# Two attention layers and two routed expert layers on one core: statistics behind the first maximum, a query product by halves, the sums of batch 3 later, and the lane tiles of the second routing on VectorE

## The reference, cut to what matters

```python
x = x + L0_xattn(layernorm(x), ctx)   # one head; softmax over ctx, a second softmax over the row maxima
x = x + L0_ffn(layernorm(x))          # 12 gates, 8 experts of 256 -> 512 -> 256 (silu), top 2
x = x + L1_xattn(layernorm(x), ctx)   # 4 heads of 64, mask, softmax over 1024, Wo
x = x + L1_ffn(layernorm(x))          # 8 experts of 256 -> 1024 -> 256 (gelu), top 2

# L1_xattn
q = layernorm(x) @ Wq;  k, v = split(ctx @ Wkv)
a = softmax(where(mask, q @ k.T * 64 ** -0.5, -inf));  out = (a @ v) @ Wo

# both ffn blocks: route by the two largest of logits = layernorm(x) @ gate
out = sum over the 2 experts picked of gate_weight * expert(layernorm(x))
```

## Time and profile before

| | |
|---|---|
| median of 3 runs | 990.28 us (989.05 to 993.0) |
| the profiled execution, time / span | 988.45 us / 986.4 us |
| mean granted clock of TensorE in it | 0.965 |
| busy share of PE, DVE, ACT, POOL | 90%, 63%, 54%, 44% |

### The profile page before, as it was taken

The page is one execution under the profiler, slowest core; times in us unless marked ns, Lnnn a source line. Parts: engine busy times, 40 slices in busy tenths (PEclk is TensorE's granted clock), DMA queues, the critical chain, the costliest instruction groups (busy, mean ns, idle before and its releaser), DMA issues. The chain is left out here.

```text
span 986.4 us, 19692 instructions
## 1 busy us (share of the span) xinstructions
PE 891.9 (90%) x6194; PEld 788.2 (80%) x6195; DVE 624.0 (63%) x1390; ACT 527.9 (54%) x1131; POOL 431.4 (44%) x374
## 2 busy tenths in 40 slices
PE   5899999858999997689999998986799999999995
PEld 4798988737999986478787787875389999999995
DVE  6975452585666666778787787866565444544452
ACT  5644140453444443686686776656755554555452
POOL 1474341006566663664263462210145555555542
PEclk9999999979999999889999999997799999999998
DMA  9631000457676739410010100009946666666762
GB/s 302 229 96 43 1 1 1 135 202 256 222 230 237 255 112 238 86 44 23 22 44 22 44 1 2 27 1 285 324 157 198 184 211 207 199 189 203 210 187 35
DMA packets 70707, 134.74 MB, mean 137 GB/s; under 512 B 8144, under 2 KB 52816, under 8 KB 65520
## 3 DMA queue, kind: packets, MB, share of 16 engines
q1 hardware_dynamic: 57296, 110.27, 33.7%
q0 software_dynamic: 13344, 23.63, 10.2%
HBM read 109.08 MB, written 21.64 MB: 133 GB/s over the span
## 5 line engine op out<-in xcount | busy, mean ns | idle before, releaser
L1840 ACT ACTIVATE x<-d_hps,b 128x128 f32<-128x128 f32 x312 | 89.0, 367 | 114.3 <-PE d_hps L1942 114.1
L1942 PEld LDWEIGHTS d_hps<-d_xg_t,d_xw 128*128 128x128 f32 x1248 | 145.1, 192 | 2.4 <-issue 1.0
L1942 PE MATMUL d_hps<-d_xg_t,d_xw 128*128 128x128 f32 x1248 | 145.5, 275 | 0.8 <-issue 0.8
L887 POOL TENSOR_SCALAR c_prob<-c_prob,c_rinv 128x1024 f32<-128x1024 f32 x64 | 72.0, 1142 | 125.3 <-DVE c_rinv L1348 124.9
L1952 PE MATMUL d_yps<-d_w,d_hid_hi 128*128 x312 | 115.2, 402 | 0.8 <-DVE d_hid_lo L2135 0.8
L1748 POOL DMA_INDIRECT out_x<-d_y,d_take_slot x39 | 63.6, 1630 | 106.2 <-DMA out_x<-d_y,d_take_slot 82.9
L2126 DVE TENSOR_SCALAR d_xg_t<-d_take,ln_w,ln_b 128x128 f32<-128x128 f32 x78 | 28.4, 406 | 93.0 <-PE d_take L1931 92.8
L1355 DVE TENSOR_TENSOR c_pt_lo<-c_tp,c_pt_hi 128x512 fp32r<-128x512 f32 x128 | 82.1, 682 | 5.2 <-ACT c_pt_hi L1177 4.9
L1341 DVE CUSTOM_DVE_ANT_0 c_prob<-c_sc,c_minf 128x1024 f32<-128x1024 f32 x64 | 75.6, 1218 | 11.3 <-PE c_sc L974 11.2
L1177 ACT ACTIVATE c_pt_hi<-c_tp 128x512 fp32r<-128x512 f32 x128 | 69.8, 597 | 22.1 <-PE c_tp L987 21.7
L987 PE MATMUL c_tp<-const,c_prob 128*128 128x128 f32 x512 | 70.5, 281 | 12.0 <-DVE c_pt_lo L1355 11.9
(11 more groups left out here) (377 smaller groups left out, 2209.5 us busy)
## 6 DMA issues: line engine op xcount, KB each, us to landing
d_xw<-in_w SPq DMA_DIRECT2D x39, 1024.0 KB
b_w<-in_w SPq DMA_DIRECT2D x47, 512.0 KB, 7.7
d_w<-in_w SPq DMA_DIRECT2D x8, 1024.0 KB, 12.0
a_raw<-in_ctx_t SPq DMA_DIRECT2D x8, 512.0 KB, 7.2
a_raw<-in_ctx SPq DMA_DIRECT2D x8, 512.0 KB, 4.5
ybuf<-a_zero SPq DMA_DIRECT2D x2, 2048.0 KB, 12.5
k_stage<-in_ctx_t SPq DMA_DIRECT2D x12, 256.0 KB, 3.2
rows<-b_xn_all SPq DMA_DIRECT2D x1, 2048.0 KB, 12.8
```

The lines of the kernel that those rows point to most:

```text
L887: nc.gpsimd.tensor_scalar(prob[w][:], prob[w][:], rinv[:, w:w + 1], 1.0, ALU.mult, ALU.mult).then_inc(s["prob_ready"], 1)
L1840: op = nc.scalar.activation(hid[q][:, h * FH + c, :], src[:, c, :], ACT.Gelu_apprx_tanh, bias=b1[:, ds(e, 1), h * FH + c])
L1942: mm = nc.tensor.matmul(hps[j % 2][h][:, c * P:(c + 1) * P], w1[j % WL][:, k, at:at + P], xg_t[j % 2][:, k, :], start=(k == 0), stop=(k == ...
```

## The change

Five edits. In attention0, `maximum(0, 0)` moves ahead of the last four `bn_stats`, the variance behind `invert(0, 0)`, the inverse deviation behind `maximum(0, 2)`, and ACT's root behind `exponential(0, 1)`. In attention1, SP waits for the second half of batch 0's rows before it loads batch 1's; 17 unread matmuls stand in place of 22; `q_proj(0)` starts with the first half of `xn_lo`; `scores(0, 0)` starts with the high part of q. The statistics of batch 3 move behind `low_parts(0, 2, 1)`; `head_sum(0, 0)` takes a wait on `sum_d3`, since it writes where a transfer reads. In the second routing, DVE makes all 32 lane tiles, `value_parts` is `val0` alone and stands after `low_out(2)`, and `weights_low(5)` stands ahead of the first `take_in`.

```diff
@@ attention0, scalar
-                root(REST, 13)
-
                 exponential(0, 0)
                 exponential(0, 1)
+                root(REST, 13)
                 high_parts(0)
@@ attention0, vector
                 for t in range(TB, T):
+                    if t == T - TB:
+                        maximum(0, 0)
                     nc.vector.bn_stats(m.bn[:, t, :], m.x[:, t, :]).then_inc(s["bn_done"], 1)
-                dve.wait_ge(s["bn_done"], T)
-                stats_chain(nc, m, dve, s["stat"], s["sqrt_done"], REST, 7, 2)
-
-                maximum(0, 0)
                 maximum(0, 1)
                 invert(0, 0)
+                dve.wait_ge(s["bn_done"], T)
+                variance(nc, m, dve, s["stat"], REST, 7)
                 invert(0, 1)
                 maximum(0, 2)
+                inverse_std(nc, m, dve, s["stat"], s["sqrt_done"], REST, 7, 2)
                 norm_enc(1)
@@ attention1, sync
             sp.wait_ge(e["x_ready"], T)
+            sp.wait_ge(s["y0_in1"], 32)
             for k in range(2):
                 load_y(1, k)
@@ attention1, tensor: q_proj
-            def q_proj(c, bank):
+            def q_proj(c, bank, ahead=False):
                 cs = slice(c * P, (c + 1) * P)
-                three_passes(bank, [(wq_hi[:, k, cs], wq_lo[:, k, cs], xn_hi[:, k, :], xn_lo[:, k, :])
-                                       for k in range(KD)]).then_inc(s["q_done"], 1)
+                for k in range(KD):
+                    if ahead:
+                        pe.wait_ge(s["xn_lo"], k + 1)
+                    pairs = three(wq_hi[:, k, cs], wq_lo[:, k, cs], xn_hi[:, k, :], xn_lo[:, k, :])
+                    for n, (lhs, rhs) in enumerate(pairs):
+                        mm = nc.tensor.matmul(bank, lhs, rhs, start=(k == 0 and n == 0), stop=(k == KD - 1 and n == 2))
+                mm.then_inc(s["q_done"], 1)
@@ attention1, tensor: scores
-                    pe.wait_ge(s["q_lo"], b * KD + hp + 1)
+                    pe.wait_ge(s["q_lo" if b or u else "q_hi"], b * KD + hp + 1)
...
                     for n, (qx, kx) in enumerate(three(q_hi, q_lo, k_hi, k_lo)):
+                        if b == 0 and u == 0 and n == 2:
+                            pe.wait_ge(s["q_lo"], 1)
@@ attention1, tensor: front
-            for _ in range(22):
+            for _ in range(17):
                 nc.tensor.matmul(tp[0][:], ctx_hi[:, 0, 0:P], ctx_hi[:, 0, 0:S], start=True, stop=True)
...
-            pe.wait_ge(s["xn_lo"], KD)
             pe.wait_ge(s["v_lo"], 4)
-            q_proj(0, xb[:])
+            q_proj(0, xb[:], ahead=True)
@@ attention1, vector, unit 3
                 if b == 0:
+                    dve.wait_ge(s["sum_d3"], 16)
+                head_sum(b, 0)
+                low_parts(b, 2, 1)
+                if b == 0:
                     summed(3)
                     dve.wait_ge(s["x_bn"], B)
                     variance(nc, m, dve, s["stat"], cols(1, B - 1), 7)
-                head_sum(b, 0)
-                low_parts(b, 2, 1)
@@ experts
-    LANES_ACT = 8
+    LANES_ACT = 8 if first else 0
@@ experts, scalar
                                      ).then_inc(s["val0_ready"], 1)
+                if not LANES_ACT:
+                    return
...
             for e in PE_LOW[:2]:
                 low_out(e)
-            value_parts()
+                if e == (PE_LOW[1] if first else PE_LOW[0]):
+                    value_parts()
@@ experts, vector
+            if not first:
+                weights_low(DVE_LAST[0])
             take_in(0, 0)
             take_in(1, 1)
-            for e in DVE_LAST:
+            for e in DVE_LAST[0 if first else 1:]:
                 weights_low(e)
```

## The result

The changed kernel takes **983.72 us** (median of 20 runs, 979.47 to 991.97), the kernel before 991.75 us (median of 20, 986.36 to 996.34). The ratio is 0.9932, 95% interval 0.9915 to 0.9949: about 6.7 us, 5.1 to 8.4, are gone (8.0 between the two medians). The forecast's difference was 3.4 us; the measured one is about twice that. The base moved too: I started from the median of three runs, 990.28, and that of 20 is 991.75, 1.5 us more.

The account below looks back on a forecast made before the run. PE, busy 90% of the span, was taken to bound the kernel, so only its idle time counts. Terms -0.9 + 1.5 - 0.9 - 3.1 = -3.4 took the profiled 988.45 to 985.05, median 986.8 us; range 982.8 to 990.2.

Parts of the forecast that it names:

- Attention0: Attention0: PE's turn of tile 2 comes 0.9 to 1.0 us earlier, kept to the end; -0.9 us, bounds 0 and -2.1.
- SP's wait: Front of attention1: later loads of batches 1 to 3 delay the first adding transfer; +1.5 us, bounds 0 and +7.4.
- the rival in which the transfers eat all: Attention1: first transfer waits for all SP's loads (+3.0), second slows (+4.4); 992.8 us, kernel slower; chance 0.06.
- The query's edits: Front of attention1: first scores end 1.9 us earlier, but DVE then waits for the transfer at summed(1); gain 0.
- Unit 3: Batch 0 of attention1: head sum and low parts run in DVE's wait, unit 4's exponential earlier; -0.9 us, bounds 0 and -1.45.
- Second routing: Second routing: slots end earlier, weights_low(5) helps, the clock takes some back; -3.1 us, bounds -4.3 and -1.4.
- Lanes and clock: Second routing: DVE's lane tiles bring -3.95 us, a low clock after PE's new 3.1 us idle costs 1.2.
- `weights_low(5)`: Second routing: run early under PE's wait, it cuts PE's later 0.79 us wait to about 0.5; -0.3 us.
- the kind case: Rival: no clock drop in the routing (-1.2 more) and a transfer that doesn't mind the loads (-1.5 more); 984.1 us; chance 0.31.
- The tables' case: Rival in attention0: a table switch costs twice its load, 2.56 us, making that term +1.7; 989.4 us; chance 0.03.

Follow-up runs that it names:

- part_unit3: The kernel before with only the sums of batch 3 moved behind head sum and low parts in unit 3: 988.95 us against 992.23, ratio 0.9974.
- the parts: Four kernels, each the kernel before with one area's edits alone: attention0 0.9952, front of attention1 0.9965, unit 3 0.9974, second routing 0.9943.
- front_loads: The kernel before with only SP's wait on batch 0's second half added ahead of the later loads: ratio 0.9995.
- fill_unit3: The kernel before with 18 unread matmuls in PE's idle 4.66 us in unit 3 of batch 0: 992.18 us, ratio 1.0004.
- late_low5: The changed kernel with weights_low(5) of the second routing back behind take_in: 983.98 us, ratio 0.9916 to the kernel before.
- same_again: The kernel before, unchanged, timed once more as a control: 991.89 us against 992.93, ratio 0.9996.

## Why the prediction was right, and where it was not

Its time was right, its working in half of the terms, and the time in part by luck. The same sum from the 991.75 us of 20 runs would have given 988.3, with a range of 984.3 to 991.7, and the measured 983.72 lies below that. The forecast's difference was half of the measured one. By steps:

1. **Attention0, -0.9.** The mechanism is as told, turn for turn, and the third exponential at 26.00 for 26.3. The size was low: 1.7 us by the means at the end of attention0, because the turn of tile 2 keeps 1.55 us, and because the clock no longer falls on the scores (twice in eight traces before, never in six). 0.8 us are left at the first experts, so the term as summed holds, but by two errors that cancel: I had said that a gain kept at the end of this stretch shows in full at the end.
2. **SP's wait, +1.5.** This is the step that failed. It rested on reading as "the adding transfer hardly runs while SP's loads run", and so on its waiting for the loads to drain. But in that trace it was issued at 380.7 us, and its first packet comes 2.8 to 4.4 us after the issue in every trace; from then on it runs beside the loads. With these started some 4 us later it did not come later: `summed(1)` is 0.7 us earlier by the means of six and eight traces. So the cost of 1.5 us isn't there, and the rival in which the transfers eat all fell with it; that the wait gains is shown by means alone, of traces that overlap a little.
3. **The query's edits, 0.** Right: in six of the seven traces that have them, DVE stands 1.4 to 3.3 us ahead of `summed(1)` for the transfer. But once they are in, a gain of the transfer shows, and I never priced a gain on that side of the tie.
4. **Unit 3, -0.9.** The mechanism is right, and so is the size: 0.8 us from the landing, by the mean of six traces; the new wait was 4.1 us for 3. What was missing is the clock behind it: with the idle 4.66 us gone from its place, PE ran the stretch behind `x_norm` at 1.00 in five traces of six, where it had not in five of seven. That is another 1.7 us in part_unit3, and 1.3 by the means of the whole change's four traces and the unchanged four (234.4 and 235.7 us). I had looked for a clock's price only where the change adds idle time, in the routing, and not for what it gives back where it takes idle time away, although had shown that such waits cost.
5. **Second routing, -3.1.** Lanes and clock: -2.75 forecast, -3.0 measured at the first `d_hps`, by the means; the low stretch came where it was said and took 1.6 us, near to the 1.7 that I had put at 2 chances in 3 (1.2). `weights_low(5)`: -0.3 forecast, -1.0 measured. I had kept 0.5 us of PE's wait for a late gelu; there is none.

Added up anew, by means: -0.8 for attention0; in attention1 -1.2 for the last adding transfer, which lands at 52.3 and not 53.5 us (0.6 of it stand at `summed(1)` already), -0.8 for the reorder and -1.3 for the clock, together the -3.3 that the stage shows (305.2 for 308.5); -4.4 for the routing at its last `d_hps` (means 292.0 and 296.4). That makes -8.5 by the stages, at the edge of what timing gives, -5.1 to -8.4. Of the rivals, the kind case (984.1) came closest in time. Of its two premises one held, that the transfer doesn't mind the loads; the other, no drop of the clock in the routing, did not. The tables' case is out by the rows at 19.69 and 26.00.

Open: why the parts' ratios add up to more than the whole's, and attention0's to more than its marks; why batch 3's first transfer is shorter; and how often the clock stays low in the router, as told below.

## What to carry to other kernels

Where two chains end in a tie, price the edits of both sides together: at the tie each alone is worth nothing, and both are worth the smaller of the two gains. Take a queue's silence for a wait only after comparing it with the time from issue to first packet elsewhere. A wait of PE costs its length and often what the clock takes behind it, so look at the stretch behind each wait that an edit makes or removes, and where work ends in front of a transfer, try a filler there. And where unchanged stages scatter by more than the effect, compare marks inside the changed stage, over several traces, before believing a span.

## What the runs showed that I had not expected

In three of the 14 traces (front_loads, fill_unit3, late_low5) the clock stays at 0.50 for some 31 us, through the whole router of the second routing, though PE is busy without a gap from 676 to 692 us in front_loads. In the other 11 it falls in the router too, but only 11 to 15 us behind the first `d_tpx`. PE in front_loads, then in before (us, busy, PEclk, DMA share, GB/s):

```profile
680.00:684.00 4.00, 4.00 (x21) 0.50 1.10 349
684.00:688.00 4.00, 4.00 (x20) 0.50 1.10 348
688.00:692.00 4.00, 4.00 (x21) 0.50 1.10 348
```

```profile
675.00:679.00 4.00, 3.93 (x35) 1.00 1.10 363
679.00:683.00 4.00, 3.81 (x31) 0.93 1.09 344
```

Eight logit matmuls take 1.71 us there and 0.96 in before, and a pair of tiles comes every 2.75 us and not every 1.44:

```profile
678.05 1.71 PE L1881 MATMUL d_lps<-d_gw,d_xn_t 128*128 128x8 f32 x8
...
680.80 1.71 PE L1881 MATMUL d_lps<-d_gw,d_xn_t 128*128 128x8 f32 x8
```

```profile
675.66 0.96 PE L1880 MATMUL d_lps<-d_gw,d_xn_t 128*128 128x8 f32 x8
...
677.10 0.96 PE L1880 MATMUL d_lps<-d_gw,d_xn_t 128*128 128x8 f32 x8
```

The slots end 7 us later in the two with the old routing (44.6 us for 37 to 38) and 8 in the one with the new (41.2 for 32.4 to 33.5). It came in two kernels that had nothing changed in this stage, and their profiled executions took 996.8 and 997.6 us, so it is likely one source of the runs at 995 us and above; same_again's 997.3 us has another. Single runs of the kernel before reach from 986 to 999.5 us. More warming matmuls in the router would be the next thing to try; this was not run, and what sets this off is not known.
